# Two GNN layers on one core: the second layer's product taken in the other order

## The chip, the cores and the metric

The kernel runs on one NeuronCore of a Trainium2 chip. Its time is the device time of one execution in microseconds (us); the lower, the better. Several executions were timed and one more was profiled.

## The reference

Eight graphs (batches) of 1024 nodes with 256 features each; `adj` is a dense 1024 x 1024 matrix per batch. Per batch:

```python
h = relu(layernorm(x))
# layer 0: attention weights from two score vectors, three hops folded into the weights Wk[0..2]
Xw = h @ Wv + bv; sj, si = Xw @ aw[:256], Xw @ aw[256:]
T  = adj * exp(leaky_relu(sj[None, :] + si[:, None] + ab));  T = T / rowsum(T)
x  = x + relu(h @ Wk[0] + T @ (h @ Wk[1]) + T @ (T @ (h @ Wk[2])) + biases)
# layer 1
h  = relu(layernorm(x));  Ah = adj + I;  dh = rsqrt(rowsum(Ah))
out = x + relu(dh * (Ah @ (dh * h @ kernel)) + bias)
```

## The kernel before

Rows of nodes are tiled by 128, so a batch has 8 tiles (`NT`); features make two blocks of 128 (`KD`). All products are done in float32r with each operand split into a high part (rounded) and a low part (what rounding left), as three matmuls per product: high x high, high x low, low x high. So each operand needs a rounding by ACT (`..._hi`) and a subtraction by DVE or POOL (`..._lo`).

Each engine has its own program, written out by hand, and semaphores link them. PE's program for batch b (`batch`, line 1043) has these stages:

- **U**: eight chunks of T @ g2 (24 matmuls each, 256 or 258 columns; `accumulate`, lines 1029 to 1031). At its end the first transposes of the next batch.
- **dense 0** of batch b + 1 (`layer0_dense`): transposes of the normalised `h0` (L896), products with the weights (L904, 512 and 258 columns) and `si` rows.
- **V**: eight chunks of T @ g1, of the same form as U. Inside it two of layer 1's transposes.
- **layer 1 dense** (`layer1_dense`): per tile of nodes 6 matmuls of 256 columns, h against W (`wl`). It needs the transpose of `h1` (four groups of four 128-column transposes per batch: `layer1_transposes`, L896).
- **Z**: eight chunks of Ah @ y (`z_chunk`, again lines 1029 to 1031: 24 matmuls of 256 columns each with tiles of the adjacency, `a_hi`/`a_lo`, as weights, and y = `g1_hi`/`g1_lo` moving).

The names that the change touches: DVE's `norm1` normalises two tiles into `h1` (L587, with `rstd1` from POOL's `power`, L322); ACT's `transposed_hi` and DVE's `transposed_lo` split the transposed tiles (`ht_hi`, `ht_lo`); ACT's `l1_scaled` (L429) and DVE's `l1_low` (L704) move the dense result out of PSUM, scaled by `dh`; ACT's `a_round` (L441) and DVE's `a_low` (L663) split half a chunk of the adjacency, 128 x 512; DVE's `z_chunk` (L712, L717) makes an output tile in two steps, and SP's `stores` sends it. `o_tile` has two buffers, so an output tile waits for the store of the one before the last.

Beside its own batch, ACT and DVE prepare T of the next one, in eight units of 128 x 1024: `leaky` (L393, four instructions), `exponent` (L399), DVE's `t_prod` (L652), ACT's `t_high` (L407), DVE's `t_low` (L657). Tables of numbers such as `HIGH_Z`, `LEAKY_Z` and `PROD_V` say after which chunk of which stage a unit's step stands. ACT, DVE and POOL run their instructions strictly in the order written, so a step that waits holds up all that stands behind it.

## Time and profile before

| what | value |
|---|---|
| median of 3 runs | 801.88 us (801.55 to 802.0) |
| the profiled execution | 801.45 us |
| its span, first to last instruction | 799.5 us |
| PE busy | 784.4 us, 98% of the span |
| weight loads (PEld) | 756.0 us, 95% |
| DVE busy | 638.6 us, 80% |
| ACT busy | 515.5 us, 64% |
| POOL busy | 129.4 us, 16% |
| one batch in the middle of the program | about 96.5 us |

The span is cut into the instructions' own times. A matmul's duration in the profile is longer than the distance to the next one, because matmuls overlap; what a matmul costs is the distance between starts. The same holds in part for ACT and DVE, whose neighbours overlap a little.

### The profile page before, as it was taken

How to read it: one execution, taken by the hardware profiler on the slowest of the kernel's cores; microseconds unless marked ns; L12 is line 12 of the kernel's file. 1: busy time of each engine (PE TensorE's matmuls, PEld its weight loads, DVE VectorE, ACT ScalarE, POOL GpSimd, SP SyncE). 2: the span in 40 equal slices, each digit the busy share in tenths (PEclk: the TensorE clock that was granted, in tenths of full speed). 3: DMA queues.
4: the chain of work that ended last, by engine and by line, in shares of the span. 5: the costliest groups of instructions: out<-in, count | busy, mean ns of one | idle time of the engine just before them, and what ended most of it. 6: DMA issues, size and time to landing. Idle time of an engine off the chain costs nothing.

```text
span 799.5 us, 15983 instructions
## 1 busy us (share of the span) xinstructions
PE 784.4 (98%) x6142; PEld 756.0 (95%) x6142; DVE 638.6 (80%) x1544; ACT 515.5 (64%) x987; POOL 129.4 (16%) x120
## 2 busy tenths in 40 slices
PE   8798999999999999999999999999999999999998
PEld 8597999989999899998999999999999999999998
DVE  6985889868897688976989679896798868895676
ACT  3986766757576676666667567665776657667142
POOL 1032010311104111030201402023010220103200
PEclk9999999999999999999999999999999999999999
DMA  7555435843278251772527625284343842356403
GB/s 240 221 156 170 139 117 177 274 144 134 66 224 295 75 171 54 244 258 67 194 70 250 214 73 192 75 297 156 126 140 128 287 127 99 100 182 234 158 9 106
DMA packets 64492, 128.71 MB, mean 161 GB/s; under 512 B 5536, under 2 KB 31520, under 8 KB 64416
## 3 DMA queue, kind: packets, MB, share of 16 engines
q1 hardware_dynamic: 55648, 97.01, 37.1%
q10 hardware_dynamic: 8768, 30.68, 11.5%
q8 instruction: 49, 0.80, 0.4%
q14 instruction: 27, 0.22, 0.1%
HBM read 119.28 MB, written 8.39 MB: 160 GB/s over the span
## 4 chain that ended last, share of the span: by engine, by line
PE 91%; ACT 4%; DVE 4%; issue 1%; DMA 0%; POOL 0%; SPq 0%; DVEq 0%; ACTq 0%
PE acc L1029 22%; PE acc L1031 22%; PE acc L1030 22%; PE da L904 13%; PE db L904 6%; PE tp L896 3%; ACT tg_e L393 1%; PE acc L924 1%; ACT t_hi L407 1%; ACT tg_e L399 1%; DVE h L587 1%; DMA h<-x_dram 0%; DVE g_tmp L677 0%; DVE ht_lo L606 0%; ACT a_raw L424 0%
## 5 line engine op out<-in xcount | busy, mean ns | idle before, releaser
L1029 PE MATMUL acc<-g_hi,t_hi 128*128 128x256 f32 (+1 forms) x1024 | 293.0, 286 | 2.7 <-DVE g_lo L632 2.7
L1031 PE MATMUL acc<-g_hi,t_lo 128*128 128x256 f32 (+1 forms) x1024 | 289.9, 283 | 0.0
L1030 PE MATMUL acc<-g_lo,t_hi 128*128 128x256 f32 x1024 | 288.7, 282 | 0.0
L1029 PEld LDWEIGHTS acc<-g_hi,t_hi 128*128 128x128 f32 x1024 | 193.9, 189 | 3.1 <-issue 3.1
L1030 PEld LDWEIGHTS acc<-g_lo,t_hi 128*128 128x128 f32 x1024 | 194.3, 190 | 0.0
L1031 PEld LDWEIGHTS acc<-g_hi,t_lo 128*128 128x128 f32 x1024 | 194.1, 190 | 0.0
L1029 PE MATMUL acc<-g_hi,a_hi 128*128 128x256 f32 x512 | 145.5, 284 | 0.1
L1030 PE MATMUL acc<-g_lo,a_hi 128*128 128x256 f32 x512 | 144.0, 281 | 0.0
L1031 PE MATMUL acc<-g_hi,a_lo 128*128 128x256 f32 x512 | 144.0, 281 | 0.0
L327 POOL TENSOR_TENSOR g_lo<-g_tmp,g_hi 128x256 fp32r<-128x256 f32 x64 | 60.6, 947 | 353.0 <-ACT g_hi L449 353.0
L393 ACT ACTIVATE tg_e<-si,sij 128x256 f32<-128x256 f32 x256 | 109.4, 501 | 12.9 <-DVE t_lo L657 10.2
L441 ACT CAST a_hi<-a_raw 128x512 fp32r<-128x512 f32 x128 | 78.7, 621 | 49.3 <-PE acc L1031 46.0
L322 POOL TENSOR_TENSOR rstd<-ve,mhalf 128x2 f32<-128x2 f32 (+2 forms) x41 | 54.6, 1332 | 271.4 <-DVE ve L576 270.5
L1029 PEld LDWEIGHTS acc<-g_hi,a_hi 128*128 128x128 f32 x512 | 96.4, 188 | 1.8 <-DVE g_lo L704 1.8
L1030 PEld LDWEIGHTS acc<-g_lo,a_hi 128*128 128x128 f32 x512 | 96.4, 188 | 0.0
L1031 PEld LDWEIGHTS acc<-g_hi,a_lo 128*128 128x128 f32 x512 | 96.3, 188 | 0.0
L663 DVE TENSOR_TENSOR a_lo<-a_raw,a_hi 128x512 fp32r<-128x512 f32 x128 | 84.6, 686 | 8.0 <-ACT a_hi L441 7.7
L407 ACT CAST t_hi<-t_raw 128x1024 fp32r<-128x1024 f32 x50 | 52.4, 1049 | 26.5 <-DVE t_raw L652 26.4
L399 ACT ACTIVATE tg_e<-tg_e 128x1024 f32<-128x1024 f32 x64 | 68.1, 1064 | 1.2
L449 ACT CAST g_hi<-g_tmp 128x256 fp32r<-128x256 f32 x64 | 26.0, 407 | 66.3 <-DVE g_tmp L677 65.5
L424 ACT ACTIVATE a_raw<-a_raw 128x1024 f32<-128x1024 f32 x64 | 67.4, 1053 | 0.5 <-DMA a_raw<-adj_dram 0.5
L652 DVE TENSOR_TENSOR t_raw<-tg_a,tg_e 128x1024 f32<-128x1024 f32 x50 | 61.1, 1222 | 3.9 <-ACT tg_e L399 3.1
(129 smaller groups left out, 1424.3 us busy)
## 6 DMA issues: line engine op xcount, KB each, us to landing
a_raw<-adj_dram SPq DMA_DIRECT2D x64, 512.0 KB, 4.5
a_raw<-adj_t_dram SPq DMA_DIRECT2D x64, 512.0 KB, 4.9
tg_a<-adj_t_dram ACTq DMA_DIRECT2D x58, 512.0 KB, 4.0
x_res<-x_dram SPq DMA_DIRECT2D x64, 128.0 KB, 3.6
out_dram<-o_tile SPq DMA_DIRECT2D x64, 128.0 KB, 3.0
h<-x_dram SPq DMA_DIRECT2D x7, 1024.0 KB, 5.3
tg_a<-adj_t_dram SPq DMA_DIRECT2D x6, 512.0 KB, 3.5
h<-x_dram SPq DMA_DIRECT2D x4, 256.0 KB, 4.0
```

The lines of the kernel that those rows point to most:

```text
L327: nc.gpsimd.tensor_tensor(g1_lo[:, i, :], g1_tmp[:, i % 2, :], g1_hi[:, i, :].bitcast(F32), ALU.subtract).then_inc(g1_ready, 1)
L393: ins = nc.scalar.activation(tg_e[:, s, :, q, :], si[:, c].rearrange("p (s i) -> p s i", s=2), ACT.Prelu, bias=sij[:, jt, 0:1], alpha=SLOPE)
L399: nc.scalar.activation(tg_e[:, u % TS], tg_e[:, u % TS], ACT.Exp).then_inc(e_ready, 1)
L407: nc.scalar.copy(t_view(t_hi, u), t_parts(b, u)).then_inc(t_hi_done, 1)
L424: nc.scalar.activation(a_raw[:, t % RS, :], a_raw[:, t % RS, :], ACT.Copy, accum_out=row_a[:, t:t + 1]).then_inc(rows_done, 1)
L441: nc.scalar.copy(a_half(a_hi, i, h), a_raw[:, i % RS, h * N // 2:(h + 1) * N // 2]).then_inc(a_hi_done[h], 1)
L652: nc.vector.tensor_tensor(t_parts(b, u), tg_a[:, s], tg_e[:, s], ALU.mult).then_inc(prod_ready, 1)
L663: nc.vector.tensor_tensor(a_half(a_lo, i, h), a_raw[:, i % RS, h * N // 2:(h + 1) * N // 2], a_half(a_hi, i, h).bitcast(F32), ALU.subtract ...
L904: ins = nc.tensor.matmul(dst[:, 0:n], l, r, start=(c == 0 and a == 0), stop=(c == len(pairs) - 1 and a == 2))
L1029: nc.tensor.matmul(acc[:, s, 0:n], l_hi, r_hi, start=(jt == 0), stop=False)
L1030: nc.tensor.matmul(acc[:, s, 0:D], l_hi, r_lo, start=False, stop=False)
L1031: ins = nc.tensor.matmul(acc[:, s, 0:n], l_lo, r_hi, start=False, stop=(jt == NT - 1))
```

## The change

Layer 1 computes W-last: first Zt = (Ah @ hs) transposed, then Zt against W. For this, h is scaled by `dh` as it is normalised, and the scaled h (`hs_hi`, `hs_lo`) is the weights operand, while a half row of the adjacency chunk, 512 columns, moves. PE's Z stage is now 16 pieces (`layer1_piece`) of 6 matmuls of 512 columns. Pieces 0 to 7 fill `zt[0]` (the banks of `da`), pieces 8 to 15 `zt[1]` (those of `tp`). ACT's `zt_high` and DVE's `zt_low` split each half of Zt into `ht_hi`/`ht_lo`, and `out_product` (6 matmuls of 256 columns with W moving) makes an output tile: four after the pieces 10 to 13 of Z, four after chunks 1 to 4 of the next batch's U (or at the very end in the last batch). The transposes of layer 1, `norm1`, `l1_scaled` and `l1_low` go. The bias of the norm (`nb1`) is a small DVE step, and the norm itself moves to ACT (`hs_high`: two activations, two roundings), with the low part on POOL (`hs_split`). The norm of layer 0 moves from DVE to ACT as well (`norm0`). SP's stores and loads are put in another order, `h0` is loaded in four parts (its memory is shared with `hs_hi`), and a second copy of the adjacency (`adj_z`) gives the chunks in the layout that a piece needs. New tables place the steps of the next batch's T.

```diff
     SCORE_V = {-1: 1, 2: 2, 3: 3, 5: 4}
-    HIGH_V = {1: (0, 1), 5: (2,), 7: (3,)}
-    PROD_V = {0: 1, 3: 2, 5: 3}
-    LOW_V = {1: 0, 2: 1}
-    LEAKY_Z, EXP_Z = {0: 5, 4: 6, 6: 7}, {0: 5, 5: 6, 6: 7}
-    HIGH_Z, HIGH_U = {3: 4, 5: 5}, {0: 6, 1: 7}
...
+    HIGH_V = {1: (0, 1), 5: (2,)}
+    PROD_V = {0: 1, 3: 2, 5: 3, 7: 4}
+    LOW_V = {1: 0, 2: 1, 6: 2}
+    LEAKY_Z, EXP_Z = {3: 5, 6: 6, 11: 7}, {4: 5, 7: 6, 12: 7}
+    HIGH_Z, HIGH_U = {0: 3, 5: 4, 9: 5, 13: 6}, {0: 7}
+    PROD_Z, PROD_U = {5: 5, 9: 6, 14: 7}, {}
+    LOW_Z, LOW_U = {1: 3, 6: 4, 10: 5, 15: 6}, {1: 7}
...
-    STATS_U = {0: (0,), 1: (1, 2), 2: (3, 4), 3: (5, 6), 4: (7,)}
-
-    DIAG_Z = {0: 4, 1: 5, 2: 6, 3: 7}
-
-    A_FIRST = {i: (i + 2, 1) for i in (0, 2, 3, 4, 5)} | {1: (4, 0)}
-    A_THEN = {0: (3, 1)} | {i: (i + 3, 0) for i in (2, 3, 4)}
+    STATS_U = {0: (0, 1), 1: (2, 3), 2: (4, 5), 3: (6, 7)}
+
+    DIAG = (0, 1, NT - 2, NT - 1)
+    DIAG_Z = {7: NT - 2, 9: NT - 1}
+    NP = 2 * NT
+    OUT_Z = {10 + i: i for i in range(HJ)}
+    OUT_U = {1 + i: HJ + i for i in range(HJ)}
...
-        h0 = sb("h0", [P, NT, D])
-        h1 = sb("h1", [P, 2, 2, D])
+        at = (nc.sbuf_base + 31) // 32 * 32
+        sb("h_space", [P, NT, D])
+        h0 = nc.alloc_sbuf_tensor_at("h0", [P, NT, D], F32, offset=at)
+        hs_hi = nc.alloc_sbuf_tensor_at("hs_hi", [P, NT, D], F32R, offset=at)
+        hs_lo = sb("hs_lo", [P, NT, D], F32R)
...
-        g1_tmp = sb("g1_tmp", [P, 2, D])
+        tmp = sb("tmp", [P, 2, D])
...
-        l1_bank = [da[:, 0, :], da[:, 1, :], db[:, :]]
-        LB = len(l1_bank)
-        U_PHASE, V_PHASE, Z_PHASE = 0, 1, 2
+        out_bank = [db[:, :], da[:, 0, :], da[:, 1, :]]
...
+        zt = [da, tp.rearrange("p g k c -> p g (k c)")]
+        zt_hi, zt_lo = (part.rearrange("p g k c -> p g (k c)") for part in (ht_hi, ht_lo))
...
-            def load_h0(b):
-
-                sp.wait_ge(tp0_full, b * NG)
-                sp.dma_start(h0[:, :, :], x_v[b]).then_inc(h0_loaded, 16)
+                             adj_z[b, i]).then_inc(raw_loaded[i % RS], 16)
+
+            def load_h0(b, g):
+
+                if b > 1:
+                    sp.wait_ge(piece_done, (b - 2) * NP + NT + 2 * g + 2)
+                else:
+                    sp.wait_ge(tp0_full, NG)
+                sp.dma_start(h0[:, 2 * g:2 * g + 2, :], x_v[b, :, 2 * g:2 * g + 2]).then_inc(x0_loaded[g], 16)
...
-
-            load_h0(1)
+                load_chunk(b, RS + 2)
+                load_chunk(b, RS + 3)
+                if left > 0:
+                    rows(b + 1, (0, 1))
+                for g in range(NG):
+                    if left > 1:
+                        load_h0(b + 2, g)
+                    if g < 2 and left > 0:
+                        rows(b + 1, (g + 2,))
+                    if g == 1:
+                        stores(b, 0)
+                        stores(b, 1)
+                    if g == 2:
+                        stores(b, 2)
+                        stores(b, 3)
+
+            for g in range(NG):
+                load_h0(1, g)
             rows(0, range(RS))
...
+            def hs_split(b, t):
+
+                pool.wait_ge(hs_hi_done, b * NT + t + 1)
+                nc.gpsimd.tensor_tensor(hs_lo[:, t, :], tmp[:, t % 2, :], hs_hi[:, t, :].bitcast(F32),
+                                        ALU.subtract).then_inc(hs_ready, 1)
...
                     power(rstd1, ve1, ve1_ready, b * NG + g + 1, rstd1_ready, slice(2 * g, 2 * g + 2))
+                    hs_split(b, 2 * g)
+                    hs_split(b, 2 * g + 1)
 
...
+            def norm0(b, g):
+
+                if g == 0:
+                    act.wait_ge(nb0_ready, b)
+                for t in (2 * g, 2 * g + 1):
+                    nc.scalar.activation(h0[:, t, :], h0[:, t, :], ACT.Relu, bias=nb0[:, t:t + 1],
+                                         scale=rstd0[:, t:t + 1]).then_inc(h0_ready, 1)
+
+            def hs_high(b, par, g):
+
+                act.wait_ge(nb1_ready, b * NG + g + 1)
+                if g > 0:
+
+                    act.wait_ge(hs_ready, b * NT + 2 * g)
+                for t in (2 * g, 2 * g + 1):
+                    nc.scalar.activation(tmp[:, t % 2, :], p0[:, par, t, :], ACT.Relu, bias=nb1[:, t:t + 1],
+                                         scale=rstd1[:, t:t + 1]).then_inc(h1_ready, 1)
+                for t in (2 * g, 2 * g + 1):
+                    act.wait_ge(h1_ready, b * NT + t + 1)
+                    nc.scalar.copy(hs_hi[:, t, :], tmp[:, t % 2, :]).then_inc(hs_hi_done, 1)
+
+            def zt_high(b, r):
+
+                for f in range(KD):
+                    if f == KD - 1:
+                        act.wait_ge(piece_done, b * NP + (r + 1) * NT)
+                    else:
+                        act.wait_ge(zt_full, 2 * b + r + 1)
+                    nc.scalar.copy(zt_hi[:, f, :], zt[r][:, f, :]).then_inc(zt_hi_done, 1)
...
-
-                    act.wait_ge(diag_done, b * NT + i + 1)
-
-                if i >= 2 and h == 0:
-                    act.wait_ge(z_half_full, b * NT + i - 1)
-                elif i >= 2:
-                    act.wait_ge(acc_full, b * PHASES + 2 * NT + i - 1)
+                if h == 0 and i in DIAG:
+
+                    act.wait_ge(diag_done, b * len(DIAG) + DIAG.index(i) + 1)
+                elif h == 0:
+                    act.wait_ge(raw_loaded[i % RS], 16 * (b * (2 * NT // RS) + NT // RS + i // RS + 1))
+
+                if i >= 2:
+                    act.wait_ge(piece_done, b * NP + 2 * (i - 2) + h + 1)
...
+                    if i in (2, 4, 6):
+                        hs_high(b, par, i // 2 - 1)
...
+                for q in range(NP):
+                    if q == NP // 2:
+                        zt_high(b, 0)
+                    if q + 4 < NP:
+                        a_round(b, (q + 4) // 2, q % 2)
+                    if q == 1:
+                        hs_high(b, par, NG - 1)
+                    if not last:
+                        if q in HIGH_Z:
+                            t_high(b + 1, HIGH_Z[q], b + 2 == B)
+                        if q in LEAKY_Z:
+                            leaky(b + 1, LEAKY_Z[q])
+                        if q in EXP_Z:
+                            exponent(b + 1, EXP_Z[q])
+                if last:
+                    zt_high(b, 1)
...
+            def moments1(b, g):
+
+                count, c = b * NG + g + 1, slice(2 * g, 2 * g + 2)
+                dve.wait_ge(stats1, count)
+                for t in (2 * g, 2 * g + 1):
+                    ins = nc.vector.bn_aggr(mv1[:, t, :], st1[:, t, :])
+                ins.then_inc(mean1, 1)
+                dve.wait_ge(mean1, count)
+                nc.vector.scalar_tensor_tensor(out=ve1[:, c], in0=mv1[:, c, 1], scalar=EPS_LN, in1=row_a1[:, c],
+                                               op0=ALU.add, op1=ALU.mult).then_inc(ve1_ready, 1)
...
+            def zt_low(b, r):
+
+                for f in range(KD):
+                    dve.wait_ge(zt_hi_done, (2 * b + r) * KD + f + 1)
+                    nc.vector.tensor_tensor(zt_lo[:, f, :], zt[r][:, f, :], zt_hi[:, f, :].bitcast(F32),
+                                            ALU.subtract).then_inc(zt_ready, 1)
...
+            def out_chunk(b, par, i):
                 s = i % 2
 
-                dve.wait_ge(acc_full, b * PHASES + 2 * NT + i + 1)
-                nc.vector.scalar_tensor_tensor(out=z_tmp[:, s, :], in0=acc[:, acc_slot(Z_PHASE, i), 0:D], scalar=dh[:, i:i + 1],
+                dve.wait_ge(out_full, b * NT + i + 1)
+                if i == 0:
+                    dve.wait_ge(dh_ready, b + 1)
+
+                dve.wait_ge(stored[s], 16 * (b * (NT // 2) + i // 2 + 1))
+                nc.vector.scalar_tensor_tensor(out=o_tile[:, s, :], in0=out_bank[i % OB][:, 0:D], scalar=dh[:, i:i + 1],
                                                in1=bias1[:, :], op0=ALU.mult, op1=ALU.add).then_inc(z_tmp_done, 1)
-                dve.wait_ge(z_tmp_done, b * NT + i + 3)
-
-                dve.wait_ge(stored[s], 16 * (b * (NT // 2) + i // 2 + 1))
-                nc.vector.scalar_tensor_tensor(out=o_tile[:, s, :], in0=z_tmp[:, s, :], scalar=0.0,
+                dve.wait_ge(z_tmp_done, b * NT + i + 1)
+                nc.vector.scalar_tensor_tensor(out=o_tile[:, s, :], in0=o_tile[:, s, :], scalar=0.0,
                                                in1=p0[:, par, i, :], op0=ALU.max, op1=ALU.add).then_inc(o_ready, 1)
...
+                for q in range(NP):
+                    if q == NP // 2:
+                        zt_low(b, 0)
+                    if q + 4 < NP:
+                        a_low(b, (q + 4) // 2, q % 2)
+                    if q == 0:
+                        bias1_of(b, NG - 1)
+                    if q - 1 in OUT_Z:
+                        out_chunk(b, par, OUT_Z[q - 1])
+                    if q in DIAG_Z:
+                        diag(b, DIAG_Z[q])
+                    if not last:
+                        if q in PROD_Z:
+                            t_prod(b + 1, PROD_Z[q])
+                        if q in LOW_Z:
+                            t_low(b + 1, LOW_Z[q])
+                if last:
+                    zt_low(b, 1)
+                    for i in range(HJ, NT):
+                        out_chunk(b, par, i)
...
+            def layer1_piece(b, q):
+
+                i, h = q // 2, q % 2
+                r, jt = i // HJ, q % NT
+                pe.wait_ge(a_ready[h], b * NT + NT + i + 1)
+                if r == 0:
+                    pe.wait_ge(hs_ready, b * NT + jt + 1)
+                a = slice(h * HJ, (h + 1) * HJ)
+                r_hi, r_lo = (part[:, i % 2, a].rearrange("p q i -> p (q i)") for part in (a_hi, a_lo))
+                for f in range(KD):
+                    l_hi, l_lo = hs_hi[:, jt, f * P:(f + 1) * P], hs_lo[:, jt, f * P:(f + 1) * P]
+                    nc.tensor.matmul(zt[r][:, f, :], l_hi, r_hi, start=(jt == 0), stop=False)
+                    nc.tensor.matmul(zt[r][:, f, :], l_hi, r_lo, start=False, stop=False)
+                    ins = nc.tensor.matmul(zt[r][:, f, :], l_lo, r_hi, start=False, stop=(jt == NT - 1))
+                    if f == KD - 1:
+                        ins.then_inc(piece_done, 1)
+                    elif jt == NT - 1:
+                        ins.then_inc(zt_full, 1)
+
+            def out_product(b, t):
+
+                pe.wait_ge(zt_ready, KD * (2 * b + t // HJ + 1))
+                if t >= OB:
+
+                    pe.wait_ge(z_tmp_done, b * NT + t - OB + 1)
+                c = slice(t % HJ * P, (t % HJ + 1) * P)
+                split_product(out_bank[t % OB], D, [(zt_hi[:, f, c], zt_lo[:, f, c], wl_hi[:, f, :], wl_lo[:, f, :])
+                                                    for f in range(KD)]).then_inc(out_full, 1)
...
-
-                layer1_dense(b, 0, last)
-                layer1_transposes(b, 2)
-                layer1_dense(b, 1, last)
-                layer1_dense(b, 2, last)
-                layer1_transposes(b, 3)
-                z_chunk(0, range(HJ))
-                z_chunk(1, range(HJ))
-                layer1_dense(b, 3, last)
-                z_chunk(0, range(HJ, NT))
-                z_chunk(1, range(HJ, NT))
-                for i in range(2, NT):
-                    z_chunk(i)
-
+
+                dense = b + 1 if last else b + 2
+                pe.wait_ge(g2_ready, dense * NT)
+                pe.wait_ge(p0_ready, dense * NT)
+                pe.wait_ge(ht0_ready, dense * NG)
+                for q in range(NP):
+                    layer1_piece(b, q)
+                    if q in OUT_Z:
+                        out_product(b, OUT_Z[q])
+                if last:
+                    for t in range(HJ, NT):
+                        out_product(b, t)
 
             pe.wait_ge(ident_ready, 1)
...
     adj_t = adj.reshape(B, nt // 2, 2, P, 2, nt // 2, P).transpose(0, 1, 4, 6, 2, 5, 3)
+    adj_z = adj.reshape(B, 2, N // 2, nt // 2, 2, P).transpose(0, 1, 3, 5, 4, 2)
...
```

On PE, at the end of layer 1's dense part of the first batch and the start of Z, before (L904 is the dense product, L896 a transpose, `g` is y, `a` the adjacency):

```order
L904 MATMUL db<-wl_hi,ht_hi 128x256
L904 MATMUL db<-wl_lo,ht_hi 128x256
L904 MATMUL db<-wl_hi,ht_lo 128x256
L896 MATMUL tp<-ident,h 128x128 [waits h1_ready]
L896 MATMUL tp<-ident,h 128x128 x3
L1029 MATMUL acc<-g_hi,a_hi 128x256 [waits a_ready0,y_ready,v_tmp_done]
L1030 MATMUL acc<-g_lo,a_hi 128x256
L1031 MATMUL acc<-g_hi,a_lo 128x256
```

And with the change, on PE at piece 10 of the same stage and the first output product (L1061 to L1063 are a piece, L959 the product with W):

```order
L1061 MATMUL tp<-a_hi,hs_hi 128x512 [waits a_ready0]
L1062 MATMUL tp<-a_lo,hs_hi 128x512
L1063 MATMUL tp<-a_hi,hs_lo 128x512
L1061 MATMUL tp<-a_hi,hs_hi 128x512
L1062 MATMUL tp<-a_lo,hs_hi 128x512
L1063 MATMUL tp<-a_hi,hs_lo 128x512
L959 MATMUL db<-wl_hi,ht_hi 128x256 [waits zt_ready]
```

The transposes are gone, the matmuls are twice as wide, and the product with W now stands behind a wait for the split Zt.

On ACT with the change, from V's last steps into Z, first batch (L399 is the norm's activation, L403 the rounding of hs, L496 `a_round`, L467 `t_high`, L453 `leaky`, L459 `exponent`, L412 `zt_high`):

```order
L496 CAST a_hi<-a_raw 128x512 [waits piece_done]
L399 ACTIVATE tmp<-p,nb,rstd 128x256 [waits hs_ready,nb1_ready]
L399 ACTIVATE tmp<-p,nb,rstd 128x256
L403 CAST hs_hi<-tmp 128x256 [waits h1_ready] x2
L496 CAST a_hi<-a_raw 128x512 [waits piece_done,raw_loaded3]
L496 CAST a_hi<-a_raw 128x512 [waits piece_done]
L453 ACTIVATE tg_e<-si,sij 128x2x128 [waits prod_ready]
```

and, with two more L496, one `exponent` and one `t_high` in between, its continuation up to the rounding of Zt:

```order
L496 CAST a_hi<-a_raw 128x512 [waits piece_done,raw_loaded1]
L453 ACTIVATE tg_e<-si,sij 128x2x128 [waits si_ready,prod_ready]
L453 ACTIVATE tg_e<-si,sij 128x2x128 x3
L496 CAST a_hi<-a_raw 128x512 [waits piece_done]
L459 ACTIVATE tg_e<-tg_e 128x1024 [waits leaky_done]
L412 CAST ht_hi<-da 128x512 [waits zt_full]
L412 CAST ht_hi<-da 128x512 [waits piece_done]
```

Before, ACT had at this place the dense results' scaling (L429) and two roundings of transposed tiles (L352). Now the last pair of norms, six roundings of the adjacency and five steps of the next batch's T stand between the end of V and the rounding of Zt.

## Rows read from the trace of the kernel before

**Rows 1.** The page: busy time of the engines, and the chain that ended last.
```profile
PE 784.4 (98%) x6142; PEld 756.0 (95%) x6142; DVE 638.6 (80%) x1544; ACT 515.5 (64%) x987; POOL 129.4 (16%) x120
...
PE 91%; ACT 4%; DVE 4%; issue 1%; DMA 0%; POOL 0%; SPq 0%; DVEq 0%; ACTq 0%
```
**Rows 2.** Windows of V and of layer 1: length, PE, PEld, DVE, ACT, POOL, clock, DMA.
```profile
279.90:303.60 23.70, 23.70 (x201) 23.70 (x201) 20.83 (x49) 16.68 (x28) 4.88 (x3) 1.00 0.50 166
303.60:333.80 30.20, 30.18 (x253) 29.80 (x252) 26.80 (x54) 19.90 (x37) 0.70 (x1) 1.00 0.39 125
```
**Rows 3.** PE's timeline at a group of transposes: start us, duration us, instruction.
```profile
308.60 0.60 PE L896 MATMUL tp<-ident,h 128*128 128x128 f32 x4
308.96 0.36 PE L1029 MATMUL acc<-g_hi,a_hi 128*128 128x256 f32 x1
309.16 0.28 PE L1030 MATMUL acc<-g_lo,a_hi 128*128 128x256 f32 x1
```
**Rows 4.** PE's timeline in the last Z stage, two matmuls that are 27 apart.
```profile
790.33 0.28 PE L1031 MATMUL acc<-g_hi,a_lo 128*128 128x256 f32 x1
...
793.53 0.28 PE L1031 MATMUL acc<-g_hi,a_lo 128*128 128x256 f32 x1
```
**Rows 5.** The chain in order of time, six dense matmuls of 512 columns (two places).
```profile
171.69 1.39 PE da L904 x6
...
357.55 1.40 PE da L904 x6
```
**Rows 6.** PE's timeline where Z waits for the dense result.
```profile
314.26 0.28 PE L1031 MATMUL acc<-g_hi,a_lo 128*128 128x256 f32 x1
314.56 0.38 PE L1029 MATMUL acc<-g_hi,a_hi 128*128 128x256 f32 x1
```
**Rows 7.** ACT's timeline in Z: start us, duration us, instruction.
```profile
315.21 0.62 ACT L441 CAST a_hi<-a_raw 128x512 fp32r<-128x512 f32 x1 [1.23 <-PE acc L1031]
315.74 1.71 ACT L393 ACTIVATE tg_e<-si,sij 128x256 f32<-128x256 f32 x4
317.35 0.60 ACT L441 CAST a_hi<-a_raw 128x512 fp32r<-128x512 f32 x1
317.86 1.06 ACT L399 ACTIVATE tg_e<-tg_e 128x1024 f32<-128x1024 f32 x1
318.82 1.29 ACT L441 CAST a_hi<-a_raw 128x512 fp32r<-128x512 f32 x2
```
**Rows 8.** Groups of ACT and POOL: line, operation, count, busy us, mean ns of one.
```profile
L327 POOL TENSOR_TENSOR g_lo<-g_tmp,g_hi 128x256 fp32r<-128x256 f32 x64 | 60.6, 947 | 353.0 <-ACT g_hi L449 353.0
L407 ACT CAST t_hi<-t_raw 128x1024 fp32r<-128x1024 f32 x50 | 52.4, 1049 | 26.5 <-DVE t_raw L652 26.4
L352 ACT ACTIVATE ht_hi<-tp 128x512 fp32r<-128x512 f32 x60 | 35.6, 593 | 23.5 <-PE tp L896 22.7
L449 ACT CAST g_hi<-g_tmp 128x256 fp32r<-128x256 f32 x64 | 26.0, 407 | 66.3 <-DVE g_tmp L677 65.5
L429 ACT ACTIVATE g_hi<-da,dh 128x256 fp32r<-128x256 f32 x48 | 22.7, 475 | 30.3 <-PE da L904 30.0
```
**Rows 9.** DVE's timeline from V's last chunk to the variance of its pair.
```profile
303.86 0.47 DVE L683 SCALAR_TENSOR_TENSOR p<-acc,rinv,p 128x256 f32<-128x256 f32 x1
...
305.83 0.17 DVE L576 TENSOR_SCALAR ve<-mv 128x2 f32<-128x2 f32 x1
```
**Rows 10.** POOL's timeline, the third and fourth `power` of a batch.
```profile
299.70 1.64 POOL L322 TENSOR_TENSOR rstd<-ve,mhalf 128x2 f32<-128x2 f32 x1 [4.10 <-DVE ve L576]
306.08 0.70 POOL L322 TENSOR_TENSOR rstd<-ve,mhalf 128x2 f32<-128x2 f32 x1 [4.73 <-DVE ve L576]
```
**Rows 11.** A group of DVE, `transposed_lo`: it reads a bank of PSUM.
```profile
L606 DVE SCALAR_TENSOR_TENSOR ht_lo<-tp,ht_hi 128x512 fp32r<-128x512 f32 x60 | 41.3, 688 | 20.0 <-ACT ht_hi L352 19.4
```
**Rows 12.** The program's end: the last matmul and the last store.
```profile
796.02 0.28 PE L1031 MATMUL acc<-g_hi,a_lo 128*128 128x256 f32 x1
...
797.31 0.33 SPq L254 DMA_DIRECT2D out_dram<-o_tile  x1
```

274 lines of the change are left out of this document (92 added, 182 removed).

## The prediction

> **What bounds the kernel now.** I read the page first, then the chain of waits, then windows of one batch's stages, and last the timelines of PE, ACT and DVE around layer 1. PE is busy for 98% of the span and makes up 91% of the chain that ended last [rows 1]. In layer 1 it is busy for 30.18 of 30.20 us [rows 2]. So PE's own instructions set the time, and an edit elsewhere counts only if it makes PE wait. ACT is busy for 16.68 of 23.70 us in V and 19.90 of 30.20 us in layer 1, DVE for 20.83 and 26.80 [rows 2]: covers, but not wide ones.
>
> **What PE loses.** The change takes away four groups of transposes per batch. A group starts at 308.60 and the matmul behind it at 308.96; the next but one starts 0.20 later, where matmuls of this form stand 0.12 apart [rows 3]. A group thus costs 0.36 + 0.08 = 0.44 us, and 4 x 8 of them 14.1 us.
>
> The product with the adjacency keeps its columns and halves its matmuls: 192 of 256 columns per batch become 96 of 512. Twenty-seven matmuls take 793.53 - 790.33 = 3.20 us, 0.1185 each [rows 4]; 1536 of them are 182.0 us. Six of 512 columns with the same pattern of high and low parts take 1.39 to 1.40 us, 0.2325 each [rows 5]; 768 are 178.6 us. That is 3.4 us less; bounds are 2.8 (all six-groups at 1.40) and 4.2 (all at 1.39). The products with W stay at 48 of 256 columns per batch. Once per batch Z waits for the dense result: 0.30 us instead of 0.12 between two starts [rows 6], and the first matmul after a wait is slow by 0.08, as behind the transposes. That wait goes: 8 x 0.26 = 2.1 us. Together PE gives up **19.6 us**.
>
> A rule says that this is too little. The Trainium skill ("Perfetto Trace Analysis", Identifying the Most-Contended Engine) wants TensorE judged by the busy share of its weight loads, and here that is 95% [rows 1]; the change halves the loads of this product. The same skill ("TensorE: Matmul & The Clock Gate", Back-to-back issue gap) gives 216 ns for 512 columns, by which the 768 would take 165.9 us and the gain would be 16.1 us in place of 3.4. The rows speak against it: doubling the columns per load takes the distance from 0.1185 to 0.2325, so nothing is waiting for loads that could be freed. I keep the rows, and the rule as a rival.
>
> **What is moved to ACT, DVE and POOL.** DVE loses both norms, the dense results' low parts and four transposed low parts, and gains four `zt_low` of the size of [rows 11] and small bias steps; it has room. The new pressure is on ACT. I walk its queue from the end of V (time 0), for a batch that also prepares T of the next one.
>
> 1. The last pair of norms needs V's chunk 7: DVE's three steps and the pair's moments end 306.00 - 303.86 = 2.1 us after it [rows 9], then POOL's `power`: 0.70 us alone, 1.64 us where DVE worked beside it [rows 10]. Before it in POOL's queue now stand two `hs_split`, 0.95 us each like the present splits [rows 8]; their hs comes from ACT's third pair, which ACT reaches about when V ends. So the pair's bias is there at 3.6 (splits already done) to 5.0 (splits first, slow `power`); I take 4.4, the middle, since both happen beside DVE's `t_prod`.
> 2. The pair itself is two activations with two per-partition operands and two roundings. The nearest rows are 0.475 (one such operand) and 0.407 [rows 8]; without overlap 1.76, with neighbours overlapping by 0.1 about 1.4. I take 1.5: end at 5.9.
> 3. Then, all before the rounding of Zt: six `a_round`, two `leaky`, two `exponent`, one `t_high`. The timeline gives the distances between starts: 0.53, 1.61, 0.51, 0.96 [rows 7], and 0.95 for `t_high` (1.05 less the same overlap [rows 8]). Sum 6 x 0.52 + 2 x 1.61 + 2 x 0.96 + 0.95 = 9.2 us: 15.1.
> 4. `zt_high` twice (0.59 each, 0.07 of the first overlapped [rows 8]) and the second `zt_low` (0.69 [rows 11]) with two semaphores: 1.9 us. Zt is split at **17.0**.
>
> PE has by then done pieces 0 to 10 in 11 x 1.395 = 15.35 us, and stands before `out_product(0)`. It waits 1.6 us. The bounds by the ends above: 3.6 + 1.4 gives 0.7 us, 5.0 + 1.76 gives 2.6 us. I take **1.6 us** in each of seven batches: 11.2 us. The last batch prepares nothing and doesn't wait.
>
> Here the Trainium skill speaks against the change: "ScalarE: Activation LUTs" (What ACT_TABLE_LOAD costs) puts an ACTIVATE at 186 ns + 0.833 ns per element and about 93 ns for each per-partition pointer operand. That is 0.585 us for a norm with two pointers; the pair then takes about 1.65 us and the wait 1.75, so the sum would be 1 us longer. No row here has two pointers.
>
> Other waits of the new order are covered. The roundings of pieces 4 to 9 come 0.5 to 2.5 us before PE in the same walk. The split of the second half of Zt has U's chunks 0 and 1 as cover (5.7 us against about 4 us of DVE work and a store's wait); without it PE would wait 2 us. On SP, stores of tiles 0 to 3 now stand behind loads of adjacency rows and `h0`; `out_chunk(2)` waits for the store of tile 0, and behind it on DVE stand `t_prod(7)` and `t_low(6)`, which nobody needs before U's chunk 6. `norm0` adds four times 0.8 us to ACT in U and dense 0, where it has idle time; in the first batch, where ACT is late, it may cost 0.5 us, in the range.
>
> **The end.** Before, the last matmul starts at 796.02 and the span ends at 799.5, 3.5 later; the last store is issued at 797.31 and takes the remaining 2.2 us [rows 12]. Now PE waits after the last piece for rounding and low part, 0.3 + 0.59 + 0.69 + 0.1 = 1.7 us [rows 8, 11], and then runs four products in 2.9 us that used to stand earlier. DVE needs 0.9 us per output tile, and tile 6 waits for the store of tile 4 (2.2 us), tile 7 for tile 5: the end comes 5.5 us after the last matmul, not 3.5. The end costs 1.7 + 2.0 = **3.7 us**.
>
> **Sum.** 801.45 (the profiled execution: a span of 799.5 and 1.95 around it; the median of the runs shown is 0.4 higher) - 19.6 + 11.2 + 3.7 = 796.8, so **797 us**.
>
> **Rivals.**
> - *The rounding of Zt is in time* (chance 0.20). Then only the end is paid: 801.5 - 19.6 + 3.7 = 785.6. For it: ACT is idle for a third of layer 1 today, and the lower bounds leave only 0.7 us. Against: ACT has no idle time in steps 2 to 4.
> - *ACT becomes the bound of Z: slower* (0.22). The place is the pair of norms behind POOL's splits. If POOL's two splits and `power` each run at the slow duration beside DVE, the bias comes at 2.1 + 2 x 1.3 + 1.64 = 6.3 and not 4.4; ACT stands idle meanwhile and everything behind is late: a wait of 3.5 us per batch, 801.5 - 19.6 + 24.5 + 3.7 = 810. The change stops paying at (19.6 - 3.7) / 7 = 2.3 us per batch, inside my upper bound of 2.6.
> - *The pieces run at the skill's 216 ns* (0.05). PE gains 12.7 us more, but reaches Zt 1.1 us earlier and waits for it longer, 7.7 us of them: 792.
> - *It isn't what it says*: if the compiler kept more weight loads or matmuls per piece; the order shows 6 per piece, so none of the chance.
>
> **The numbers.** My forecast has 0.50: of that 0.44 lie below 800.2 and 0.06 near 802. With the first and third rival, faster has 0.44 + 0.20 + 0.05 = 0.69 and a little from smaller waits, 0.70; same 0.08 (0.02 from the second rival's near end); slower 0.22. A difference of 0.2% (1.6 us) is about the least that a measurement of this kernel can tell from none. The range goes from the first rival's 785 to 808, most of the second's; my forecast's own is 790 to 804.
>
> **What would show it.** Right: no transposes of layer 1; distances of 0.232 between PE's starts inside pieces; one gap of 1 to 2 us per batch, right before the first product with W in Z, released by DVE's `ht_lo`, in batches 0 to 6 and not in the last; a batch of about 95.7 us. Wrong: gaps of PE before pieces 6 to 9, released by `a_lo` or `hs_lo` (second rival); no gap at all (first); distances near 0.216 (third); or gaps in U or dense 0 that wait for `h0` or `t_lo`, of which I have none.

## The result, and the profile after

The changed kernel takes 806.7 us (median of 4 runs, 806.3 to 807.4) against 801.7 for the kernel before (801.6 to 802.0, same chip): ratio 1.0063, 95% interval 1.0048 to 1.0078. It is slower by 0.6%, where 797 was forecast. The profiled execution has a span of 804.4 us, 4.9 more than before.

The page, with the parts that answer to [rows 1], and the groups that answer to [rows 8]:

```profile
PE 771.5 (96%) x5246; PEld 709.2 (88%) x5246; DVE 592.0 (74%) x1399; ACT 556.8 (69%) x1107; POOL 180.0 (22%) x184
...
PE 61%; ACT 18%; DVE 13%; issue 4%; POOL 3%; DMA 1%; DVEq 0%; ACTq 0%; POOLq 0%
...
L352 POOL TENSOR_TENSOR hs_lo<-tmp,hs_hi 128x256 fp32r<-128x256 f32 x64 | 60.2, 961 | 81.0 <-ACT hs_hi L403 81.0
...
L399 ACT ACTIVATE tmp<-p,nb,rstd 128x256 f32<-128x256 f32 x64 | 35.0, 593 | 38.2 <-DVE nb L647 38.0
```

PE is 12.9 us less busy and yet the program is longer: the chain that ended last now leaves PE for ACT, DVE and POOL for a third of its length (it did for 8%). The weight loads' share fell from 95% to 88% and brought nothing beyond what the matmuls' own distances give. Which waits those are is in the list of waits, PE's own first (what waited, for whom: us in total, times, longest), then the one of DVE that will matter:

```profile
PE db L959 <- DVE ht_lo L775: 14.0, 7, 2.1
PE da L959 <- DVE ht_lo L674: 2.9, 1, 2.9
PE da L959 <- DVE ht_lo L775: 2.9, 2, 1.5
```
```profile
DVE o_tile L786 <- DMA out_dram<-o_tile: 30.4, 12, 5.3
```

`ht_lo` L775 is `zt_low`, the low part of Zt (it shares the tile's name). Seven waits of 1.85 to 2.09 us stand before the first product with W. One more of 1.51 us is in the U stage of one batch, before the product with the second half of Zt, and one of 1.40 at the end. The row with L674 is the first batch's wait for its first transposed pair in dense 0.

Batches, from one U stage to the next (window, length, PE busy, granted clock, DMA share):

```profile
38.80:140.83 102.03, 95.93 (x624) 0.95 0.48 160
140.83:236.69 95.86, 94.01 (x650) 1.00 0.49 163
236.69:332.71 96.02, 93.94 (x649) 1.00 0.50 165
332.71:431.88 99.17, 95.75 (x649) 0.98 0.49 162
431.88:527.73 95.85, 93.77 (x650) 1.00 0.49 163
527.73:623.61 95.88, 93.98 (x649) 1.00 0.49 165
623.61:721.17 97.56, 95.47 (x649) 0.98 0.45 152
721.17:804.40 83.23, 77.19 (x553) 0.99 0.34 110
```

and three of the kernel before, the first, the second and the last:

```profile
38.40:140.38 101.98, 98.43 (x761) 0.98 0.47 150
140.38:236.97 96.59, 96.36 (x762) 1.00 0.51 164
...
719.59:799.50 79.91, 76.70 (x642) 1.00 0.38 127
```

Four batches do nearly what was forecast: 95.85 to 96.02 us where 95.7 was said (two errors cancel there: PE gives up 0.3 us more than forecast and waits 0.6 more). The loss is in the other four, and in all of these the granted clock is below 1, in the last one only behind PE's last matmul. The first and the last window can't be set against those of before as they stand: four output products (24 matmuls, 2.8 us) now run in the next batch's U, so they left the first window and came into the last. The windows of layer 1 alone (length, PE, PEld, DVE, ACT, POOL, clock) answer to [rows 2], where it took 30.20 us:

```profile
305.14:332.71 27.57, 25.48 (x122) 20.80 (x121) 21.66 (x36) 22.88 (x43) 5.28 (x5) 1.00 0.65 219
...
402.95:431.88 28.93, 27.02 (x122) 22.03 (x121) 22.35 (x38) 22.69 (x42) 5.28 (x5) 0.94 0.64 215
...
692.05:721.17 29.12, 27.03 (x122) 22.08 (x121) 23.67 (x41) 22.87 (x43) 5.29 (x5) 0.94 0.51 175
```

The same stage takes 27.4 to 27.6 us in four batches and 28.9 to 29.1 in three. Windows of 2 us through one of these three, whose wait ends at 129.34:

```profile
126.00:128.00 2.00, 1.26 (x6) 1.00 0.13 51
128.00:130.00 2.00, 0.66 (x5) 1.00 0.78 248
130.00:132.00 2.00, 2.00 (x9) 0.66 1.04 404
132.00:134.00 2.00, 2.00 (x9) 0.50 0.84 290
134.00:136.00 2.00, 2.00 (x13) 0.99 0.60 157
```

PE idles, starts again, and then works at a granted clock of 0.50 (1.2 GHz in place of 2.4) before it is back; below, this is called half clock. It costs about 1.5 us each time (29.12 against 27.57 us for the stage).

**The whole difference.** A clean batch is 95.86 us with a gap of 2.24 between two starts where 0.23 is normal: without the wait 93.85, 2.7 less than before, 21.9 us for eight. Against this: seven gaps, 15.1 us; half clock in three of the seven stages, 4.6; the wait in one U stage, 1.7; the last batch 3.2 (1.6 of waiting for Zt, 1.4 behind the last matmul, 0.2 not traced); the first about 1.9 (a longer wait in dense 0, with half clock behind it), worked out as what its window leaves; and 0.4 before the first U stage. That makes +5.0 us; measured +4.9.

### The profile page after: what moved, and what is told of

It reads as the page before. It is cut to its first block, busy times and chain, and to the rows that moved or that the text cites. A ratio compares the mean times of both kernels' runs of the same rounds, so it can differ in the third digit from the quotient of the medians.

```text
span 804.4 us, 14243 instructions
## 1 busy us (share of the span) xinstructions
PE 771.5 (96%) x5246; PEld 709.2 (88%) x5246; DVE 592.0 (74%) x1399; ACT 556.8 (69%) x1107; POOL 180.0 (22%) x184
## 4 chain that ended last, share of the span: by engine, by line
PE 61%; ACT 18%; DVE 13%; issue 4%; POOL 3%; DMA 1%; DVEq 0%; ACTq 0%; POOLq 0%
PE da L959 14%; PE acc L1093 9%; PE acc L1095 9%; PE acc L1094 9%; PE db L959 7%; ACT tg_e L453 6%; ACT tg_e L459 3%; ACT tmp L399 3%; PE tp L1063 2%; PE tp L1061 2%; PE tp L1062 2%; POOL hs_lo L352 2%; DVE t_lo L723 2%; ACT a_hi L496 2%; DVE p L749 2%
## 5 line engine op out<-in xcount | busy, mean ns | idle before, releaser
L346 POOL TENSOR_TENSOR g_lo<-tmp,g_hi 128x256 fp32r<-128x256 f32 x64 | 55.6, 869 | 325.3 <-ACT g_hi L508 325.3
L453 ACT ACTIVATE tg_e<-si,sij 128x256 f32<-128x256 f32 x256 | 109.2, 500 | 2.7 <-DVE sij L689 2.6
L729 DVE TENSOR_TENSOR a_lo<-a_raw,a_hi 128x512 fp32r<-128x512 f32 x128 | 90.1, 720 | 22.2 <-ACT a_hi L496 21.9
L508 ACT CAST g_hi<-tmp 128x256 fp32r<-128x256 f32 x64 | 25.8, 403 | 94.1 <-DVE tmp L743 93.6
L341 POOL TENSOR_TENSOR rstd<-ve,mhalf 128x2 f32<-128x2 f32 (+2 forms) x41 | 50.4, 1229 | 178.7 <-DVE ve L643 162.2
L496 ACT CAST a_hi<-a_raw 128x512 fp32r<-128x512 f32 x128 | 77.8, 621 | 17.9 <-PE tp L1063 6.2
L352 POOL TENSOR_TENSOR hs_lo<-tmp,hs_hi 128x256 fp32r<-128x256 f32 x64 | 60.2, 961 | 81.0 <-ACT hs_hi L403 81.0
L459 ACT ACTIVATE tg_e<-tg_e 128x1024 f32<-128x1024 f32 x64 | 68.0, 1063 | 1.2
L399 ACT ACTIVATE tmp<-p,nb,rstd 128x256 f32<-128x256 f32 x64 | 35.0, 593 | 38.2 <-DVE nb L647 38.0
L723 DVE TENSOR_TENSOR t_lo<-t_raw,t_hi 128x1024 fp32r<-128x1024 f32 x50 | 61.4, 1228 | 0.0
L700 DVE TENSOR_TENSOR g_lo<-da,g_hi 128x256 fp32r<-128x256 f32 x64 | 27.1, 423 | 43.5 <-ACT g_hi L422 43.5
L467 ACT CAST t_hi<-t_raw 128x1024 fp32r<-128x1024 f32 x50 | 52.2, 1044 | 0.0
L1061 PE MATMUL tp<-a_hi,hs_hi 128*128 128x512 f32 x128 | 52.0, 406 | 0.0
L1063 PE MATMUL tp<-a_hi,hs_lo 128*128 128x512 f32 x128 | 51.9, 405 | 0.0
```

Of the source, the lines that this page charges most:

```text
L352: nc.gpsimd.tensor_tensor(hs_lo[:, t, :], tmp[:, t % 2, :], hs_hi[:, t, :].bitcast(F32), ALU.subtract).then_inc(hs_ready, 1)
L453: ins = nc.scalar.activation(tg_e[:, s, :, q, :], si[:, c].rearrange("p (s i) -> p s i", s=2), ACT.Prelu, bias=sij[:, jt, 0:1], alpha=SLOPE)
L459: nc.scalar.activation(tg_e[:, u % TS], tg_e[:, u % TS], ACT.Exp).then_inc(e_ready, 1)
L496: nc.scalar.copy(a_half(a_hi, i, h), a_raw[:, i % RS, h * N // 2:(h + 1) * N // 2]).then_inc(a_hi_done[h], 1)
L723: nc.vector.tensor_tensor(t_view(t_lo, u), t_parts(b, u), t_view(t_hi, u).bitcast(F32), ALU.subtract).then_inc(t_ready, 1)
L729: nc.vector.tensor_tensor(a_half(a_lo, i, h), a_raw[:, i % RS, h * N // 2:(h + 1) * N // 2], a_half(a_hi, i, h).bitcast(F32), ALU.subtract ...
```

## Where each loss comes from: two stages in the trace

ACT's timeline from V's end (305.14) to the rounding of Zt, batch 2:

```profile
310.04 1.10 ACT L399 ACTIVATE tmp<-p,nb,rstd 128x256 f32<-128x256 f32 x2 [1.17 <-DVE nb L647]
311.04 0.70 ACT L403 CAST hs_hi<-tmp 128x256 fp32r<-128x256 f32 x2
311.64 1.14 ACT L496 CAST a_hi<-a_raw 128x512 fp32r<-128x512 f32 x2
...
319.87 1.05 ACT L459 ACTIVATE tg_e<-tg_e 128x1024 f32<-128x1024 f32 x1
320.83 0.56 ACT L412 CAST ht_hi<-da 128x512 fp32r<-128x512 f32 x1
...
321.29 0.58 ACT L412 CAST ht_hi<-da 128x512 fp32r<-128x512 f32 x1
```

The walk of the prediction had the pair's bias at 4.4 us (4.9 here), the pair's end at 5.9 (6.6), the start of the rounding at 15.1 (15.7), and Zt split at 17.0 (17.6, when PE starts again). PE, on its side:

```profile
320.29 0.39 PE L1063 MATMUL tp<-a_hi,hs_lo 128*128 128x512 f32 x1
322.77 0.39 PE L959 MATMUL db<-wl_hi,ht_hi 128*128 128x256 f32 x1 [2.08 <-DVE ht_lo L775]
```

The bias was late for the reason given: `power` (1.61 us on POOL from 308.20) began just as the two splits ended. The estimate from the Trainium skill ("ScalarE: Activation LUTs", What ACT_TABLE_LOAD costs) was 0.585 us for a norm with two pointers, and with it about 1.65 for the pair; the rows agree, with 0.593 and 1.70 (310.04 to 311.74).

DVE's timeline over the end of layer 1 and the start of U, same batch:

```profile
327.71 0.47 DVE L786 SCALAR_TENSOR_TENSOR o_tile<-db,dh,bias 128x256 f32<-128x256 f32 x1
...
328.56 0.48 DVE L786 SCALAR_TENSOR_TENSOR o_tile<-da,dh,bias 128x256 f32<-128x256 f32 x1
...
334.82 0.48 DVE L786 SCALAR_TENSOR_TENSOR o_tile<-da,dh,bias 128x256 f32<-128x256 f32 x1 [5.32 <-DMA out_dram<-o_tile]
...
338.81 1.28 DVE L775 TENSOR_TENSOR ht_lo<-tp,ht_hi 128x512 fp32r<-128x512 f32 x2
```

`out_chunk(2)` needs the buffer of chunk 0, whose store was issued at 328.68. DVE stands still for 5.3 us, and behind it in its queue is the low part of the second half of Zt, which PE wants in U. The kernel before had the same two buffers, but its chunks came 2.84 us apart, and DVE never waited for a store:

```profile
786.21 0.48 DVE L712 SCALAR_TENSOR_TENSOR z_tmp<-acc,dh,bias 128x256 f32<-128x256 f32 x1
...
789.05 0.48 DVE L712 SCALAR_TENSOR_TENSOR z_tmp<-acc,dh,bias 128x256 f32<-128x256 f32 x1
```

Stores land in 1.7 to 6.0 us (before: 1.7 to 5.7). They did not get slower; the chunks came closer together.

## The experiments

Theories at the start: (1) ACT's queue makes the seven waits, and the idle time brings the half clock; (2) DVE, blocked by stores, is what binds, and any time won in Z is lost again in U; (3) the half clock has nothing to do with the waits. The variants ran on three chips, each with the kernel before beside them: one piece later, two pieces later, filling and stores from `p0` on the first (median of before 801.96 us); norm on DVE, ACT's queue, the three edits and Zt's rounding later on the second (801.55); both queues, fillers again and the last two on the third (801.64). Every ratio is to the kernel before on the same chip, and variants on different chips are compared by these ratios.

**Products one piece later.**
```
-    OUT_Z = {10 + i: i for i in range(HJ)}
+    OUT_Z = {11 + i: i for i in range(HJ)}
```


> The first four products with W stand one piece later (after pieces 11 to 14 of the Zt product, not 10 to 13); nothing else is changed. A, ACT's queue sets when the rounded Zt is ready and TensorE waits for it 7 times (2.05 to 2.25 us in the profile of the changed kernel): one piece is 1.39 us, so each wait falls to 0.65 to 0.85 us, 7 x 1.4 = 9.7 us less, and if the half-clock stretches behind the waits (1.5 us each, in 3 of 7) come from the idle time, up to 4.6 us more goes: 792 to 797 us. B, the output chunks on DVE and their stores are what binds (o_tile waited up to 5.3 us for a store): moved 1.4 us later they push DVE's work in the U stage back, and most of the gain is lost: 801 to 806.

Measured: 802.2 us (median of 12, 799.4 to 806.8), ratio 1.0006 (0.9994 to 1.0018). Case B. The waits in Z fell as in A, and new ones came up in U:

```profile
PE da L959 <- DVE ht_lo L775: 12.1, 8, 2.1
...
PE db L959 <- DVE ht_lo L775: 2.5, 7, 0.4
```

Six of the seven U stages now have a gap of 1.5 to 2.1 us before the product with the second half of Zt, and three of the six show half clock behind it. So PE's early arrival moved the loss from theory (1)'s place to theory (2)'s. The half clock in U comes on matmuls of 256 columns, so it doesn't need the pieces' 512.

**Two pieces later.** `OUT_Z = {12 + i: i ...}`, a last `out_chunk` behind the loop on DVE, and on ACT
```
             def zt_high(b, r):
+                if r == 1:
+                    act.wait_ge(out_full, b * NT + HJ)
```


> The same four products two pieces later (after pieces 12 to 15); ACT's first cast of the second half of Zt waits in addition until the fourth product is done. A, ACT's queue and the idle clock: no wait of TensorE is left in the Zt stage, 7 x 2.1 = 15 us less, and no half-clock stretch behind it, 4.6 us less: 786 to 789 us. A without the clock (the half-clock stretches have another cause and stay): 791 to 793. B, the stores bind: the second half's cast is 0.7 us later, chunks are 2.8 us later, TensorE waits in the U stage instead (before: once, 1.5 us): 798 or more.

Measured: 796.0 us (6 runs), ratio 0.9927 (0.9912 to 0.9942), between the cases. The wait before the product is gone and no stage of layer 1 has half clock, but PE now meets another wait, 0.95 us in each of seven batches, before piece 12 (pieces are counted from 0): its adjacency rounding stands behind Zt's on ACT and DVE. In its list of waits:

```profile
PE tp L1065 <- DVE a_lo L731: 6.7, 7, 1.0
```

**Filling the wait.** 18 transposes of the identity into a free bank ahead of PE's wait (the first wait below is for that bank).
```
             def out_product(b, t):
+                if t == 0:
+                    pe.wait_ge(v_tmp_done, b * NT + NT)
+                    warm(18)
```


> 18 transposes of the identity (0.115 us each by the warm-up rows, 2.1 us) into a free bank stand where TensorE waits for the rounded Zt; the wait itself stays. A, the half clock comes from the idle time: the waits go from 2.1 to about 0.1 us, the stage is as long as before in batches that kept the full clock (27.4 to 27.6 us) and the 3 stretches at half clock (29.1 us) vanish: 4 to 5 us less, about 802. B, the half clock comes from the load of the 512-column matmuls (or from chance): the fillers change nothing or make it more frequent: 806 to 809.

Measured: 806.4 us (5 runs), ratio 1.0051 (1.0039 to 1.0063); 0.4 less than the changed kernel (ratio 1.0063, and the intervals overlap), not 4 to 5. Yet the thing looked for happened: all seven stages take 27.4 to 27.6 us at a clock of 1.00, and the clock of the program is 0.994 to 0.997 in the five runs (0.988 to 0.990 before the edit). I had overlooked the last batch, which has no wait to fill and pays for the fillers in full:

```profile
781.58 2.13 PE L989 MATMUL acc<-ident 128*128 128x128 f32 x18
783.46 0.37 PE L959 MATMUL db<-wl_hi,ht_hi 128*128 128x256 f32 x1
```

and in this profile two U stages wait for Zt (1.2 and 0.7 us) instead of one (1.5). The time alone decides nothing here; the test is repeated below without these two faults.

**Stores that no longer hold up DVE.** The output chunk is written over the residual in `p0` and stored from there.
```
-                sp.dma_start(out_v[b, :, i], o_tile[:, i % 2, :]).then_inc(...)
+                sp.dma_start(out_v[b, :, i], p0[:, b % 2, i, :]).then_inc(...)
...
-                dve.wait_ge(stored[s], 16 * (b * (NT // 2) + i // 2 + 1))
+                if b > 0 or i > 1:
+                    dve.wait_ge(o_ready, b * NT + i - 1)
...
-                nc.vector.scalar_tensor_tensor(out=o_tile[:, s, :], in0=o_tile[:, s, :], ...
+                nc.vector.scalar_tensor_tensor(out=p0[:, par, i, :], in0=o_tile[:, s, :], ...
...
+                if b > 1:
+                    dve.wait_ge(stored[t % 2], 16 * ((b - 2) * (NT // 2) + t // 2 + 2))
                 nc.vector.tensor_tensor(p0[:, par, t, :], db[:, 0:D], bk_sum[:, :], ALU.add)
```


> The output chunk is written in place over the residual tile it adds (p0) and stored from there, so DVE no longer waits for a store to free one of the two o_tile buffers (12 waits, 30.4 us, longest 5.3 us, in the changed kernel). A, the wait on the store blocks DVE's queue, and with it the second half of the rounded Zt in one batch (TensorE waited 1.5 us at 338.4) and the last chunks at the end: 1.8 us at most in that batch, 1.5 us at the end: 803 to 805. B, these waits lie in DVE's slack: 806.5, no change.

Measured: 801.2 us (11 runs, 800.5 to 802.5), ratio 0.9992 (0.9983 to 1.0001): 5.5 less, more than A allowed. The U wait is gone, and the last batch is 1 us shorter. The rest of the profile's gain is in the clock: one stage of layer 1 with half clock and not three, and a clock of 0.991 to 0.994 in all eleven runs against 0.988 to 0.990. Why fewer waits turn into half clock here, with the seven waits in Z as long as before (14.1 us), is not explained by any run.

**The layer-0 norm back on DVE** (`norm0(b + 1, ...)` out of ACT's order; `norm0(0)` and `norm0(1)` at U's chunk 5, `norm0(2)`, `norm0(3)` in the dense stage on DVE, as before).

> The layer-0 normalization of the next batch goes back from ACT to DVE, where it stood in the kernel before; all else as changed. A, its move is worth only the first batch: there TensorE waited 2.93 us for the rounding of the first transposed pair (1.19 before) with a half-clock stretch behind it; back on DVE 1.8 us less, 804 to 805. B, DVE is short of time in the U stage (the 0.5 us norms stand ahead of the second half's Zt and the output chunks' waits): TensorE waits there in more batches, 807 to 810.

Measured: 807.7 us (6 runs, 804.3 to 808.7), ratio 1.0068 (1.0054 to 1.0083). The interval overlaps with that of the changed kernel (1.0048 to 1.0078), so no loss or gain is shown in the time; the profile has both effects. The first batch went from 102.03 to 98.36 us: PE's wait for the first pair fell from 2.93 to 1.62, and none of the three stretches of half clock that the changed kernel had in this batch came (only one of them stood behind that wait, so not all of the 3.7 us is the norm's). But PE waited in U in three batches (1.25 us at most) and not in one, and four of seven Z stages fell to half clock, behind waits of 1.88 us:

```profile
PE db L958 <- DVE ht_lo L772: 13.2, 7, 1.9
PE da L958 <- DVE ht_lo L772: 3.5, 4, 1.4
```

**ACT's queue relieved**, on top of the stores from `p0`.
```
-    LEAKY_Z, EXP_Z = {3: 5, 6: 6, 11: 7}, {4: 5, 7: 6, 12: 7}
+    LEAKY_Z, EXP_Z = {3: 5, 8: 6, 11: 7}, {4: 5, 9: 6, 12: 7}
```


> On top of the in-place stores (801.2 us): ACT's leaky and exponent of unit 6 (four at 0.43 and one at 1.0 us, 2.7 us) stand behind the casts of the first half of Zt instead of ahead of them; nothing else. A, ACT's queue makes the wait of 2.1 us at the first product with W: the casts come 2.7 us sooner, the wait goes in all 7 batches, 14.7 us less: 785 to 788. B, something else ends last (DVE's own queue, the bank, the last norm): the wait stays over 1 us: 794 to 801. In between: units 6 and 7 of the adjacency weights come 2.7 us later and hold up the V or U stage: 789 to 793.

Measured: 804.0 us (9 runs), ratio 1.0028 (1.0018 to 1.0037): 2.8 us slower than without the edit. It is case B by its mechanism, and above B's range. ACT did cast sooner, at 124.77 us where it was at 127.90 without the edit (PE reached its wait only 0.3 us sooner). But DVE's own queue was next. ACT's timeline, and then DVE's:

```profile
124.77 1.06 ACT L412 CAST ht_hi<-da 128x512 fp32r<-128x512 f32 x2
127.51 0.62 ACT L496 CAST a_hi<-a_raw 128x512 fp32r<-128x512 f32 x1 [1.68 <-DVE a_raw L770]
```
```profile
123.52 1.22 DVE L720 TENSOR_TENSOR t_raw<-tg_a,tg_e 128x1024 f32<-128x1024 f32 x1
...
125.25 1.22 DVE L725 TENSOR_TENSOR t_lo<-t_raw,t_hi 128x1024 fp32r<-128x1024 f32 x1
...
126.99 0.49 DVE L770 TENSOR_TENSOR a_raw<-a_raw,ident 128x128 f32<-128x128 f32 x2
127.39 1.28 DVE L777 TENSOR_TENSOR ht_lo<-da,ht_hi 128x512 fp32r<-128x512 f32 x2
```

The low part starts 1.6 us after the casts have ended, ACT idles meanwhile for DVE's diagonal step, and the T work that was pushed back delays the output chunks until PE waits 1.0 us for a bank. PE has two waits per batch, 1.3 and 1.0 us, in place of one of 2.0, and a batch takes 96.6 us and not 95.85; that no half clock comes inside the batches (the program's clock is 0.995 to 0.998) gives a part of it back. So without the edit ACT's queue ended last, but only some 0.7 us after DVE's (2.01 against 1.33 us of wait in the mean).

**Both queues relieved.**
```
-    PROD_Z, PROD_U = {5: 5, 9: 6, 14: 7}, {}
-    LOW_Z, LOW_U = {1: 3, 6: 4, 10: 5, 15: 6}, {1: 7}
+    PROD_Z, PROD_U = {8: 5, 10: 6, 14: 7}, {}
+    LOW_Z, LOW_U = {1: 3, 8: 4, 11: 5, 15: 6}, {1: 7}
```


> On top of the kernel with unit 6 behind Zt on ACT (804.0 us): on DVE the product of unit 5 and the low part of unit 4 (1.22 us each) go behind Zt's low halves too. A, the wait of 1.3 us that was left there is DVE's queue: ACT cast at 124.8 us and DVE subtracted only at 127.4: the low halves come 2.4 us sooner, TensorE does not wait at the first product. With the later waits (1.0 us per batch for the output bank) kept: 793 to 797; if these go too: 787 to 790. B, another wait takes its place in full because DVE and ACT have too much to do in this stage in whatever order: 801 to 805.

Measured: 793.1 us (4 runs), ratio 0.9893 (0.9880 to 0.9907): case A with the later waits kept. PE doesn't wait before the first product any more; 0.88 us per batch for the output bank are left. This shows that the seven waits come from the order of two queues, and not from too much work in the stage.

**Three edits together**: products two pieces later, stores from `p0`, norm on DVE.

> Products with W two pieces later, in-place stores, layer-0 norm on DVE. A, the three losses add: from the 796.0 us of the two-pieces-later kernel, 1.8 us in the first batch, 0.8 in one U stage and 1.5 at the end go, and the new 0.95 us wait of TensorE for the rounding of the adjacency (7 times) stays: 791 to 793. B, the store waits and these waits are the same time seen twice: 795 to 797.

Measured: 794.1 us (4 runs), ratio 0.9900 (0.9886 to 0.9915); 1.9 us better than two pieces later alone (0.9912 to 0.9942; the intervals just touch), 1.1 above A. The waits of 0.95 us remain. By the profiles, the last batch gives 0.6 us where 1.5 was expected (84.2 against 84.8), and with the norm on DVE the middle batches are 0.3 longer, 95.35 against 95.04 us.

**The same, with Zt's rounding one piece later on ACT and DVE.**
```
-                    if q == NP // 2:
+                    if q == NP // 2 + 1:
```
(at `zt_high(b, 0)` and at `zt_low(b, 0)`)

> As the kernel with all three, and the casts of the first half of Zt stand one piece later in ACT's and DVE's order (behind the adjacency rounding of piece 12). A, the 0.95 us wait is the adjacency rounding that stood behind Zt's: it goes, 7 x 0.95 = 6.7 us less than the kernel with all three: 784 to 787. B, the queue is full there, and the wait only changes its name: 0 to 2 us less.

Measured: **787.2 us** (4 runs, 787.0 to 788.8), ratio 0.9823 (0.9810 to 0.9836): case A in mechanism and size (6.9 us less than with the three edits), faster than the kernel before by 1.8%, and by 2.4% than the changed one. PE's list of waits has nothing left between the first batch and the last, where 2.2 us of waiting for Zt remain; a batch, and layer 1 of another:

```profile
134.95:229.42 94.47, 94.31 (x650) 1.00 0.49 169
...
297.90:323.91 26.01, 25.89 (x123) 20.65 (x121) 22.98 (x38) 22.51 (x42) 4.71 (x5) 1.00 0.60 214
```

**Fillers again**, on top of the stores from `p0`, and not in the last batch.

> The 18 filler transposes in the wait for the rounded Zt, on top of the in-place stores (801.2 us) and not in the last batch, where there is no wait to fill. A, idle time of about 2 us brings the half-clock stretches (granted clock 0.991 to 0.994 over the runs of the in-place kernel, against 0.996 to 0.998 where the waits were shorter): every Z stage takes 27.4 to 27.7 us, the clock is 0.996 or more, and the time 1 to 3 us less: 798 to 800. B, the half clock is chance or comes from load: stages of 28.9 us remain, clock 0.991 to 0.994, 801 to 802.

Measured: 798.6 us (5 runs, 797.4 to 799.7), ratio 0.9962 (0.9950 to 0.9975): 2.6 less than the same kernel without fillers (0.9983 to 1.0001, on another chip; the intervals don't meet). All seven stages take 27.6 us at full clock, and the clock of the program is 0.995 to 0.997:

```profile
397.72:425.31 27.59, 27.47 (x141) 1.00 0.65 218
```

PE gets nothing done in the fillers and waits for the same event, and the time falls: the half clock behind these waits comes from PE's standing still. Theory (3) is out. Why a given wait brings it and another of the same length doesn't stays open.

**The best kernel with one part undone.** First the layer-0 norm on ACT:

> The best kernel (787.2 us: products two pieces later, Zt's rounding one later, in-place stores, norm on DVE) with the layer-0 norm on ACT, as in the change. A, the move costs TensorE 1.9 us in the first batch and some half clock behind it, and nothing in the others: 789 to 791. B, it relieves DVE in the U stage (68.5 to 68.2 us): 7 x 0.25 = 1.8 us back, 787 to 788.

Measured: 789.2 us (4 runs), ratio 0.9841 (0.9827 to 0.9854). The first batch is 98.86 us (96.68 with the norm on DVE), the others 94.2 (94.5): +2.2, with one stretch of half clock more, and -0.3 for each of six batches. The last batch is 1.2 us longer (84.1 against 83.0), with half clock behind its wait of 2.24 us. The clock is 0.993 in three of the four runs and 0.997 in the fourth, the fastest at 787.3. That is A in size, with B's effect there as well; but the intervals of the two kernels overlap, so the 2 us are not clear of noise.

Then the two `o_tile` buffers:

> The best kernel with the stores from the two o_tile buffers again. A, DVE waits for stores 2 to 5 us in every batch; with the products two pieces later these waits stand just ahead of the second half of Zt: TensorE waits in the U stage in several batches, 1 to 2 us each: 790 to 797. B, the two-pieces-later order leaves slack (one wait of 0.8 us in seven batches in the first kernel of that kind): 787 to 789.

Measured: 797.2 us (5 runs), ratio 0.9940 (0.9926 to 0.9953), 10 us slower than the best: case A, at the upper end of its range. PE waits in U for the second half of Zt, as in the first experiment, and where it waited 2.06 us the clock fell. Its list of waits, and the window from 331 to 339 (PE busy, PEld, DVE, ACT, POOL, clock):

```profile
PE da L962 <- DVE ht_lo L774: 8.8, 7, 2.2
```
```profile
331.00:339.00 8.00, 5.94 (x38) 5.73 (x37) 7.32 (x18) 3.75 (x7) 1.95 (x2) 0.79 0.57 154
```

## Why the prediction was wrong

The sign was wrong, by an error of 9.7 us in the time. Point by point:

- *PE gives up 19.6 us*: right in kind, and near in size. The transposes are gone, and the distance between matmuls of 512 columns inside a piece is 0.23 us, as taken. Per batch 2.45 was forecast; 2.7 follows from a clean batch here, and 2.1 and 2.4 from batches of the best kernels, which have next to no wait (94.5 and 94.2 us). The third rival, pieces at 0.216 us, is out.
- *ACT's queue makes PE wait 1.6 us in seven batches and not in the last*: right in place, number and releaser, and short in size. It was 1.85 to 2.09 us, 2.2 between starts beyond the normal distance: 15.1 us where **11.2** stood. In the stage shown all of it is the norm pair (bias 0.5 us later, pair 0.2 longer); the nine microseconds of queue behind it were met within 0.1. That DVE's queue was nearly as late was not seen. The upper bound of 2.6 us comes to 2.5 by its own terms (5.0 + 1.76 + 9.2 + 1.9 - 15.35). One reading behind the bias was wrong: `power` was said to take 0.70 us alone and 1.64 beside DVE [rows 10], but DVE was busy beside both, with `t_prod` (299.56 to 300.79) beside the long one and with the shorter L704 and L606 (305.90 to 307.02) beside the short one. In the changed kernel it took 1.61, again beside `t_prod`.
- *Full clock behind the waits*: **this was the step that failed first.** The sum priced a wait at its own length. Three of seven waits brought half clock, 4.6 us, a term that did not exist in the sum, nor in any rival. The trace of before gave no warning in the middle batches, where PE hardly waits, but its start did: the window after PE's wait of 2.67 us that ended at 38.40 showed less than full clock too (0.66 of it from 38.4 to 42.0).
- *`out_chunk(2)` waits for a store, and nobody needs what stands behind it*: **the step that hid the most.** Behind it stands not only the T work but `zt_low` of the second half. I gave U's two chunks as its cover and named the store's wait without pricing it. In the changed kernel it cost one wait of 1.5 us, but when the products stood one piece later it took back 9 of the 11.5 us of waiting that were won in Z, and without it the changed kernel is 5.5 us and the best one 10 us faster.
- *The first batch's norm on ACT costs up to 0.5 us*: 1.9 us, the longer wait and the half clock behind it together. Four norms (2.2 us on ACT) now stand ahead of the first transposed pair's rounding, which starts at 67.22 (65.35 before).
- *The end costs 3.7 us*: 3.2, near the forecast.
- *The second rival, slower by a wait of 3.5 us*: right in sign and place, wrong in mechanism. Its own bound for paying, 2.3 us of wait per batch, was not reached (2.2); wait and half clock together, 19.7 us over seven batches, exceed it.

The errors add: 3.9 for the waits' size, 4.6 for the clock, 1.7 in U, 1.9 + 0.4 before and in the first batch, less 0.5 at the end and 2.3 for what PE gave up: 9.7 us.

## What to carry to other kernels

Price a wait of the bound engine with what follows it: on TensorE, an idle stretch of some 2 us cost about 1.5 us more than itself in 12 of 29 cases here. When a product's operand is made by two queues, walk both, and put the consumer where the slower one is ready, rather than to squeeze the queue: moving four products two pieces later, and one rounding by one, was worth more here (10.7 us for the first step) than relieving both queues (8.1), and relieving ACT alone lost 2.8. When work is bunched that used to be spread, count the buffers between it and its stores again, and look at what is queued behind the engine that waits for them.

## What the runs showed of the hardware

Half clock came behind some waits and not behind others of the same length. From layer 1 of the first batch to the U stage of the last the profiles have 29 waits of PE between 1.5 and 2.1 us, in the changed kernel and four variants; 12 have half clock behind them (3 of 7 and 0 of 1 in the changed kernel, 3 of 6 one piece later, 1 of 7 with stores from `p0`, 4 of 7 with the norm on DVE, 1 of 1 in the last variant). Behind the waits of 0.9 to 1.3 us in the kernels with products two pieces later and with relieved queues there was none, nor behind the 14 waits that were filled. Ahead of that stretch (before the first U and in the first dense 0) and in the last batch's layer 1, over all profiles, it came at none of 8 waits of 1.6 to 1.8 us, 4 of 5 of 2.2 us, 7 of 14 of 2.6 to 2.7 us and 8 of 9 of 2.9 us.

Which of the longer waits it hits is different from batch to batch, and the times of one kernel's runs go with it: the kernel with products one piece later spread over 7 us in twelve runs, its clock over 0.990 to 0.998, the fastest run with the highest clock, where the kernel before, without such waits inside a batch, spread over 1.6 us in 23.
